# Eight-core transformer kernel: the second projection unit of an attention pass is placed between its tail and its value matmuls

## The reference, cut to what matters

```python
def _L0_attn_ref(x, w_qkv, w_out, b_out, ln_gamma, ln_beta):   # HEADS = 32, DIM_HEAD = 32
    qkv = (x @ w_qkv).reshape(b, n, 3, HEADS, DIM_HEAD)
    q, k, v = transposed to (b, HEADS, n, DIM_HEAD)
    attn = softmax(einsum('bhnd,bhmd->bhnm', q, k) * DIM_HEAD ** (-0.5))
    out = einsum('bhnm,bhmd->bhnd', attn, v)
    out = out.transposed.reshape(b, n, 1024) @ w_out + b_out
    return layernorm(out) * ln_gamma + ln_beta

# layer 0
xn = layernorm(x); s = _L0_attn_ref(xn, ...); g = silu(_L0_ffn_ref(xn, ...)); x = x + s * g
# layer 1
xn = layernorm(x); s = _L1_attn_ref(xn, ...); g = silu(_L1_ffn_ref(xn, ...)); x = x + s * g
```

## Time and profile before

| what | us |
|---|---|
| runs of the kernel before (2) | 10476.04, 10374.06 |
| their median | 10425.05 |
| the profiled execution | 10468.57 |
| its span, core 2 (the slowest) | 10467.0 |
| spans of cores 0 to 3 | 10373.6, 10375.4, 10467.0, 10464.9 |
| spans of cores 4 to 7 | 10344.9, 10339.4, 10364.4, 10356.8 |

### The profile page before, as it was taken

One profiled execution on the slowest core, in us unless ns is written; L12 is line 12 of the kernel. 1 busy time (PEld: TensorE's weight loads), 2 busy tenths in 40 slices (PEclk: granted clock), 3 DMA queues, 4 the chain that ended last, 5 costly groups with the idle time before them and its releaser, 6 DMA issues.

```text
span 10467.0 us, 58601 instructions; the slowest of 8 cores (10339.4 to 10467.0 us)
## 1 busy us (share of the span) xinstructions
PE 5681.0 (54%) x17037; PEld 1761.8 (17%) x17240; DVE 3112.7 (30%) x4277; ACT 2104.5 (20%) x2326; POOL 409.7 (4%) x506
## 2 busy tenths in 40 slices
PE   2477778777853544426664444516665215835540
PEld 0122222222211111102221111102222002311110
DVE  3132222322233556311111555411111321112221
ACT  0144444444520221100000212100000110102210
POOL 0000000000000000001110000001111000000000
PEclk9866666666655555568887555557776557867765
DMA  2200000000002000135554000034453250020004
GB/s 71 44 3 0 3 3 3 3 0 0 0 20 65 3 0 0 37 67 46 46 53 98 4 0 0 4 90 43 43 51 43 90 146 28 23 64 0 0 20 140
DMA packets 508712, 356.29 MB, mean 34 GB/s; under 512 B 445968, under 2 KB 450715, under 8 KB 498162
## 3 DMA queue, kind: packets, MB, share of 16 engines
q0 software_dynamic: 441280, 160.70, 13.6%
q1 hardware_dynamic: 67122, 191.82, 5.2%
HBM read 378.92 MB, written 104.86 MB: 46 GB/s over the span
## 4 chain that ended last, share of the span: by engine, by line
PE 42%; DVE 18%; DMA 18%; ACT 13%; issue 7%; DVEq 1%; ACTq 0%; SPq 0%; POOLq 0%; POOL 0%
ACT p_at L400 8%; PE p_ps_o L419 7%; PE p_ps_out L976 3%; DMA p_w1a<-f_w 3%; DMA p_w1g<-f_w 3%; PE p_ps_a L941 3%; PE p_ps_m L1373 2%; PE p_ps_b L409 2%; PE p_ps_s L393 2%; DVE p_ssum L653 2%; DVE p_rec L738 2%; PE p_ps_g L948 2%; PE p_ps_o L729 2%; DVE p_rec L428 2%; ACT p_at L718 2%
## 5 line engine op out<-in xcount | busy, mean ns | idle before, releaser
L400 ACT ACTIVATE p_at<-p_ps_s,p_m8v 128x1024 bf16<-128x1024 f32 x1024 | 1140.8, 1114 | 1370.3 <-PE p_ps_s L393 1281.5
L393 PE MATMUL p_ps_s<-p_qT,p_kT 32*128 32x512 bf16 x2048 | 858.9, 523 | 327.2 <-ACT p_at L400 327.2
L941 PE MATMUL p_ps_a<-p_xh,p_w1a 128*128 128x512 bf16 (+1 forms) x1378 | 475.5, 503 | 546.9 <-DMA p_w1g<-f_w 475.9
L419 PE MATMUL p_ps_o<-p_at,p_vsb 128*33 128x512 bf16 x2048 | 724.7, 531 | 0.0
L428 DVE RECIPROCAL p_rec<-p_ps_o 1x512 f32<-1x512 f32 x128 | 428.7, 3349 | 539.9 <-PE p_ps_qk L329 343.0
L707 PE MATMUL p_ps_s<-p_qTb,p_kTb 64*128 64x512 bf16 x448 | 241.6, 566 | 528.2 <-ACT p_at L718 419.9
L965 DVE SCALAR_TENSOR_TENSOR p_acts<-p_ps_a,p_b1av,p_gbuf 128x512 bf16<-128x512 f32 (+1 forms) x176 | 132.1, 750 | 1146.4 <-ACT p_gbuf L961 1145.1
L718 ACT ACTIVATE p_at<-p_scr,p_m30v 128x512 bf16<-128x512 f32 x448 | 323.2, 722 | 597.2 <-DVE p_scr L713 576.2
L412 DVE COPY p_nbc<-p_ps_b 32x512 f32<-32x512 f32 x127 | 86.2, 679 | 1074.5 <-PE p_ps_b L409 1067.3
L948 PE MATMUL p_ps_g<-p_xh,p_w1g 128*128 128x512 bf16 (+1 forms) x1382 | 390.4, 430 | 2.8 <-issue 1.5
L976 PE MATMUL p_ps_out<-p_acts,p_w2sb 128*128 128x512 bf16 (+1 forms) x1376 | 348.0, 406 | 79.1 <-DVE p_xf L982 60.9
(11 more groups left out here) (254 smaller groups left out, 5921.8 us busy)
## 6 DMA issues: line engine op xcount, KB each, us to landing
p_w1a<-f_w POOLq DMA_DIRECT2D x168, 256.0 KB, 4.8
p_w1g<-f_w POOLq DMA_DIRECT2D x168, 256.0 KB, 4.2
p_xt<-x SPq DMA_DIRECT2D x32, 512.0 KB
s_xfa<-p_xf SPq DMA_DIRECT2D x16, 1024.0 KB, 3.9
p_xf<-s_xfa SPq DMA_DIRECT2D x16, 1024.0 KB
p_st<-s_s SPq DMA_DIRECT2D x32, 512.0 KB
p_w2sb<-f_w POOLq DMA_DIRECT2D x2, 5376.0 KB, 51.1
s_xnT_f<-p_ch SPq DMA_DIRECT2D x8, 1024.0 KB, 5.1
```

The lines of the kernel that those rows point to most:

```text
L393: m = ev.op("tensor", lambda e, kt=kt, pb=pb, half=half, hbase=hbase, q0=q0, tp=tp, buf=buf: e.matmul(ps_s[pb][:, half * 512:(half + 1) * ...
L400: e1 = ev.op("scalar", lambda e, pr=pr, pb=pb: e.activation(at[:, pr * 1024:(pr + 1) * 1024], ps_s[pb][:], AF.Exp, bias=m8v[:], scale=floa ...
L419: mavl = ev.op("tensor", lambda e, kt=kt, hh=hh, po=po, buf=buf: e.matmul(ps_o[po][:], vsb[buf][:, kt * 132 + hh * 33: kt * 132 + hh * 33 ...
L941: ma = ev.op("tensor", lambda e, k=k, c=c, t0=t0, buf=buf, sz=sz: e.matmul(ps_a[buf][0:sz, :], w1a[buf][:, k * 128:k * 128 + sz], xh[k][:, ...
```

## The change

Every pass now takes one unit at its head, ahead of the S matmuls, and one more between the tail of the pass before and the value matmuls, as long as `queue` holds any. The queue of 24 is therefore empty after pass 11 instead of pass 15. The mark for the weight guard is tested at both places.

```diff
--- before.py
+++ after.py
@@ -370,10 +370,8 @@
                     q0 = qc * 512
                     it = g * 16 + hh * 4 + qc
                     po = it % 2
-                    nfill = 2 if (hh * 4 + qc) < 8 else 1
-                    for _ in range(nfill):
-                        if queue:
-                            queue.pop(0)()
+                    if queue:
+                        queue.pop(0)()
                     if not queue and (g + 1) in states and not wg_set:
                         wguard[(g + 1) % 2] = ev.mark("mm")
                         wg_set = True
@@ -415,6 +413,11 @@
                             oall[tg][thb:thb + 32, tq0:tq0 + 512], ps_o[tpo][0:32, :],
                             nbc[tpo][:], ALU.mult), waits=[c1], inc="vx")
                         pending_tail = None
+                    if queue:
+                        queue.pop(0)()
+                    if not queue and (g + 1) in states and not wg_set:
+                        wguard[(g + 1) % 2] = ev.mark("mm")
+                        wg_set = True
                     for kt in range(16):
                         mavl = ev.op("tensor", lambda e, kt=kt, hh=hh, po=po, buf=buf: e.matmul(
                             ps_o[po][:], vsb[buf][:, kt * 132 + hh * 33: kt * 132 + hh * 33 + 33],
```

## The result

| | before | after |
|---|---|---|
| median of the runs, us | 10414.89 (10 runs, 10357.93 to 10525.61) | 10128.92 (12 runs, 10087.45 to 10232.82) |
| ratio | | 0.9742, 95% interval 0.970 to 0.9783 |
| stage on core 2, first to last start of the reciprocal, us | 2504.2 | 2236.2 |
| one group of 16 passes, us | 320.86 or 324.26 | 283.31 |
| Q/K doubles, us | 24.1 | 19.6 to 20.2 |

The kernel is 2.6% faster, and the stage is 268 us shorter on core 2, which is 2.6% of 10415: the whole gain is in the edited loop. The ratio compares only runs in which no die of the chip stood at a lower clock than the other for the whole kernel, so it is not quite the quotient of the two medians.

A forecast was written before the change was run, and what follows sets the result against it. PE waiting for DVE's casts behind the reciprocal was taken to bound the stage; 194 us of waits plus 39 of clock gave 233 us saved, 10195 us (2.2% faster), range 10100 to 10300.

The forecast's parts named there:

- The bound and the wait: Head of passes 0 to 7: PE's wait for the first unit's cast, behind the reciprocal, goes; 74 + 120 = 194 us.
- The new place costs no wait: Between tail and value matmuls: the first unit's cast is done by over 7 us, so the moved unit costs no wait.
- The second unit costs its high-clock time wherever it stands: Moved unit ahead of the value matmuls: charged about 1.7 us for Q/K and 0.6 us for V.
- the uncertain term: The moved unit's charge of 1.7 or 0.6 us, if it takes part of the value matmuls' slow stretch.
- only the waits go: Rival: moved unit costs in full as before, value matmuls begin at low clock; 194 us saved, 10231 us; chance 0.2.
- The size of the clock term: Edited loop: 39 us beyond the waits, from the second unit and first S matmuls at the high clock.
- the lower bounds: Shortest pass periods in a group: 19.1 us for Q/K doubles, 16.9 for V doubles, 15.7 for plain passes.
- Schedule within the group at zero: Passes 8 to 15: units finish earlier and weight loads can start some 68 us sooner; effect put at zero.
- no wait took the place of the old one: Rival at the new place: the wait moves rather than goes, about 10,425 us; chance 0.02.
- The slower rival: Value matmuls and head units: the clock no longer rises, +118 us in all, 10543 us; chance 0.03.
- the capped one: Rival: dense passes granted less than full clock, 430 us at 0.75, leaving 90 us saved, 10335 us; chance 0.03.
- The stage's end: Last reciprocal on core 2 starts near 2726 us instead of 2959.

The follow-up runs named there:

- e4: Kernel before with only DVE's order changed, the reciprocal written behind the casts of the head units: ratio 0.9812, group 296.96 us.
- e12: Changed kernel with the reciprocal computed twice, one behind the other: stage 2240.3 us, group 283.31 us, ratio 0.9664.
- e2: Changed kernel with the old counts, the second unit at the new place only in passes 0 to 7: stage 2236.2 us, ratio 0.9746.
- e8: Changed kernel with each pass's value matmuls written in pairs between the next pass's S pairs, units between them too: stage 2517.8 us, ratio 1.0015.
- e10: e8 with S matmuls over 128 rows, K in one zero-padded tile for every head: stage 1509.3 us, ratio 0.9032.
- e6: Changed kernel with none to three unneeded V-sized matmul blocks per pass in the last group: stage 2239.2 us, last group 275.5 us.
- e7: Changed kernel with the head unit's matmuls spread over the S phase, one behind each S pair: stage 2236.7 us, ratio 0.9743.
- e3: Kernel before with both units left at the head, the second writing into the broadcast's PSUM tile: stage 2259.4 us, ratio 0.9774.
- e5: e3 with all units between tail and value matmuls, none at the head: stage 2258.7 us, ratio 0.9785.
- e11: Kernel before, waits kept, with 10 or 18 extra matmuls ahead of the second head unit: stage 2473.6 us on core 2, ratio 0.996.

## Why the prediction was right, point by point

*The bound and the wait.* Right: the chain and the waits lost what was named, the 194 us are gone, and e4 shows that the reciprocal ahead of the cast made them (126 us of waits forecast, about 126 measured).

*The new place costs no wait.* Right: no wait of PE for DVE in the stage, and e12's doubled reciprocal is hidden as well.

*The second unit costs its high-clock time wherever it stands.* Right for the Q/K unit (7.3 us with the value matmuls against 5.4 to 5.6 without it): it runs at the low clock itself, and the value matmuls give the difference back. For the V unit 0.6 us was too much: a V double settles at 17.06 us, the length of a pass without any unit in the earlier trace rows, so there it costs nothing. This was the uncertain term, and its rival "only the waits go" (194 us) falls with the 268 measured.

*The size of the clock term.* Too small: 39 us were put down for all beyond the waits, 74 came (268 - 194). It was explained as the second unit and the first S matmuls at the high clock; in the table above the first S matmuls give 21 us, the value matmuls 83, and the units take 35 more than before, since the moved ones run at the low clock. The forecast group was 287.6 us, the measured 283.31, which over seven groups is 30 us. Most of the rest is that before's group was taken as 320.9 from one that was measured, while three of the six whole groups on core 2 took 324.26; in those the first single pass took 17.2 to 17.7 us, not the 16.26 from which the lower bounds were made. Inside the group, the V doubles were put at 17.3 and took 16.8 to 17.06, the plain passes at 17.0 and took 16.2 to 16.9, the Q/K doubles at 20.3 and took 19.6 to 20.2. The plain passes were read from the long run of such passes at 17.06 in the earlier trace rows; the four of a group climb from 16.2 to 16.9 and end before they get there.

*Schedule within the group at zero.* Right (e2).

*The rivals.* The clock did rise in every pass, no cap showed, and no wait took the place of the old one. The slower rival, though, was priced on the right mechanism and dismissed with a wrong reason: "denser work is unlikely to prevent" the rise. e8 is denser and prevents it. Why the changed kernel escaped, no run isolates; a reading that fits e8 and e10 is that its moved unit and the value matmuls behind it use all 128 rows, one behind the other. Two of the rivals' sums were off, too. The slower one counts 84 V units at the head, where the changed kernel has 56, so that it should say 106 us more instead of 118. The 430 us of the capped one don't come out of its terms, which give some 360. Neither enters the forecast.

*The stage's end* was forecast near 2726 us and is 2689.4; the total, 10195, stands 66 us above the 10128.92 measured, inside the range: 35 us are the clock term, 10 the median of before (10414.89 now, 10425.05 then), the rest lies within the spread of the runs.

## What to carry to other kernels

When two steps share one PSUM tile, look at what stands ahead of the cast that empties it, in the queue of the engine that does this: a late, unhurried instruction there (here a 3.35 us reciprocal) stalls the matrix engine, and moving either is nearly free. Where the granted clock falls behind idle stretches, a gap on the matrix engine costs more than its length (56 gaps of 194 us in all were worth 245 to 268) and a small saving of matmul time less than its own. Before making a matmul loop denser, look at its granted clock: if it is low and many of the matmuls are over few rows, as here, try padding them first.

## What the runs showed of the hardware

- PE busy 1394 of 1400 us at a granted clock of 0.50 (e8), and 0.99 for the same stream of columns with the S matmuls over 128 rows instead of 32 (e10). With the S matmuls, over a third of all, over 32 rows the clock stayed down from 520 to 2980 us on all eight cores; rows of zeros in K, with the moving Q full, were enough to lift it.
- Passes settle at 17.06 us with no unit and with two V units (the changed kernel), in e6 they fall towards it, and the groups of kernels with different orders of work agree to 0.01 us (283.31 in the changed kernel, e2, e6, e7 and e12; 286.72 in e3 and e5). What a pass gains or loses ahead of the value matmuls, these take back: 6.2 us behind no block of e6, 3.7 behind three.
- Matmuls that only fill a wait can pay: in e11, 784 of them (28 x 10 + 28 x 18), read by nothing, made the stage 31 us shorter on four cores and 7 to 10 us on the other four; in whole runs no gain shows (0.996, 0.9919 to 1.0001).
